# GNN kernel on one core: propagation and last layer on edge rows, sums per tile of 128 sorted edges by one-hot products, third residual step in the last propagation round, output scattered

## The chip, the cores and the metric

One Trainium2 chip, one of its NeuronCores. The metric is the device time of one execution in microseconds, median of several runs; the kernel before takes 13,499.98 us (three runs, 13,473.8 to 13,504.35). Engines: TensorE (PE), VectorE (DVE), ScalarE (ACT), GpSimd (POOL), and SyncE (SP), which here only issues transfers. Indirect DMAs, which gather or scatter 128 rows by 128 indices held in SBUF, are issued by POOL.

## The reference

50,000 nodes with 96 features, 50,000 edges sorted by destination `dst`; all in f32. Four residual layers, each on `h = relu(layernorm(x))`:

```python
x = x + L0(h)   # attention over edges: segment_sum(V[src]*score, dst) / segment_sum(score, dst)
x = x + L1(h)   # gated message network, segment_sum by dst, update network, layernorm
x = x + L2(h)   # 16 rounds of propagation, no weights:
#   deg = segment_sum(1, dst) + 1 ; norm = rsqrt(deg)[src] * rsqrt(deg)[dst], self loops included
#   g = h ; 16 times: g = 0.9 * segment_sum(norm * g[src], dst) + 0.1 * h
x = x + L3(h)   # deg3 = segment_sum(w, dst) + 1 ; dinv = rsqrt(deg3)
#   y = h @ W ; out = dinv * (segment_sum(w * (dinv*y)[src], dst) + dinv*y) + b
```

The sums by `dst` are what the change is about. About 31,600 nodes have at least one incoming edge; the others get nothing but their self loop.

## The kernel before

Rows of nodes and of edges are laid out alike: 128 partitions with 392 consecutive rows each (`P`, `CH`), so a partition holds a stretch of the sorted edges. Work goes in `NB` = 49 batches of `J` = 8 columns; one indirect DMA moves one column, that is 128 rows of 96 values, so a pass over all edges (or nodes) is 392 of them. `skewed()` writes each engine's program as ticks: in tick t a stage with lag L handles batch t - L, the stages in the order given; four batches are in flight. Between stages of the program stands a `Block`, at whose ends all engines meet.

Sums along a partition (`scan_step`, lines 344 to 359): for each of the eight columns VectorE runs two `scalar_tensor_tensor`, a running sum `S` that restarts where `dst` changes, and a sum `F` over the edges whose `dst` is that of the partition's first edge. `F` is needed where a segment crosses partitions: after the last batch a product with the matrix `B` adds up what the partitions before contribute, and 128 extra rows (`AUX`) hold it. A node finds its sum by a pointer (`ptr_i`, for layer 2 `yptr_i`), which is another gather.

The stages, with the lines that matter:

- Preparation (from 380): masks, counts and weights per edge, the slots of each segment; while layer 0's node products run, 392 scatters write `info_t` (556).
- Layer 0 and layer 1: edge stages with `scan_step`, node stages that gather the sums (`n_ag`). Layer 1's node stage (1060 to 1226) stores `x2` and the scaled `h` as the start of the propagation, in both `y_t` tables.
- First propagation step (1229 to 1345): per batch 8 gathers of neighbours' values `r_g` and 8 of the edge's own start `r_c`, scan, four VectorE instructions of 128x768; the start term goes to `c_t`, the values stay in SBUF (`H`) and go to `y_t`. An edge row holds the value of its destination node, so a round needs no read-back by nodes: row e of `y_t` is what the sum of the edges up to e gives, and only the last edge of a segment has the full one. `yptr_e` points every edge to it.
- Fifteen rounds (1347 to 1477): POOL gathers, VectorE scans, TensorE adds `H`, `c_t` and the sums in PSUM through the identity (1415, 1416, 1421), ScalarE scales by `k_e` into `H` (1443), SP stores to the other `y_t` (1381). A round begins when all rows of the last are stored (`after(pool, s_st, 16 * NB * r)`).
- Layer 3 preparation (p6, from 1480): gathers of the final values by node `n_y`, `x3 = x2 + root * y`, layernorm, product with `W`, times `dinv` into `z_t`.
- Layer 3 sums (p7): gathers `e_g` of `z_t` by `src`, times weight, scan, into `agg3_t`.
- Output (p8): gathers `n_ag` of the sums by node, plus `z`, times `dinv`, plus `x3` and `b`, stored to `out`.

What orders the rounds on the side of the gathers is this helper, and nothing else is on POOL's queue:

```python
def gathers(table, to, h, done):
    G.sem_inc(s_turn_p)
    for j in range(J):
        G.indirect_dma_start(out=to(j), out_offset=None, in_=table,
                             in_offset=bass.IndirectOffsetOnAxis(ap=idx_s[:, h, j:j + 1], axis=0)
                             ).then_inc(done, 16)
```

## Time and profile before

| | |
|---|---|
| median of the runs | 13,499.98 us |
| span of the profiled execution | 13,552.9 us |
| POOL busy | 9,980.6 us (74%) |
| VectorE busy | 6,176.6 us (46%) |
| TensorE busy, matmul | 6,161.5 us (45%) |
| ScalarE busy | 3,099.7 us (23%) |
| DMA engines, mean | 115 GB/s |

The page gives each engine's busy time and, in 40 slices, how it is spread. The groups of instructions name a line, an engine and an operation with count, busy time, mean length of one, and the idle time just before them with what ended it; "issue" means that nothing in the profile was waited for. The timeline gives single instructions with their start and length in us.

### The profile page before, as it was taken

How to read it: one execution, taken by the hardware profiler on the slowest of the kernel's cores; microseconds unless marked ns; L12 is line 12 of the kernel's file. 1: busy time of each engine (PE TensorE's matmuls, PEld its weight loads, DVE VectorE, ACT ScalarE, POOL GpSimd, SP SyncE). 2: the span in 40 equal slices, each digit the busy share in tenths (PEclk: the TensorE clock that was granted, in tenths of full speed). 3: DMA queues.
4: the chain of work that ended last, by engine and by line, in shares of the span. 5: the costliest groups of instructions: out<-in, count | busy, mean ns of one | idle time of the engine just before them, and what ended most of it. 6: DMA issues, size and time to landing. Idle time of an engine off the chain costs nothing. (4 is left out here: it accounts for less than half of the span.)

```text
span 13552.9 us, 124135 instructions
## 1 busy us (share of the span) xinstructions
PE 6161.5 (45%) x16702; PEld 3564.8 (26%) x16702; DVE 6176.6 (46%) x21955; ACT 3099.7 (23%) x11470; POOL 9980.6 (74%) x10210
## 2 busy tenths in 40 slices
PE   6422105873002555555555555555555555544000
PEld 4322103542001322223323332323322322233000
DVE  4344455596343444444444444444444444444533
ACT  5300133394000222222222222222222222233000
POOL 7677777676777777777777777777777777777777
PEclk8655557886555777777777777777777777755555
DMA  5433353374223333333333333333333333344245
GB/s 150 120 99 100 109 145 97 92 216 142 76 75 89 117 112 112 118 112 112 116 112 112 118 112 112 116 112 112 117 112 112 116 113 112 116 132 129 73 116 140
DMA packets 855833, 1558.86 MB, mean 115 GB/s; under 512 B 321698, under 2 KB 378674, under 8 KB 855666
## 3 DMA queue, kind: packets, MB, share of 16 engines
q1 hardware_dynamic: 523217, 1053.28, 22.9%
q0 software_dynamic: 332448, 504.04, 16.3%
q14 instruction: 148, 1.20, 0.0%
q8 instruction: 20, 0.33, 0.0%
HBM read 954.90 MB, written 602.08 MB: 115 GB/s over the span
## 5 line engine op out<-in xcount | busy, mean ns | idle before, releaser
L340 POOL DMA_INDIRECT r_g<-y_t,idx_s x6272 | 6051.0, 965 | 2128.7 <-issue 2115.0
L349 DVE SCALAR_TENSOR_TENSOR r_S<-r_S,scan_s,r_g 128x96 f32<-128x96 f32 x6272 | 2020.3, 322 | 4670.1 <-DMA r_g<-y_t,idx_s 3968.8
L1421 PE MATMUL r_pu<-r_S,ident 128*128 128x384 f32 x2940 | 1883.7, 787 | 3127.9 <-DVE F L351 3127.9
L1443 ACT ACTIVATE H<-r_pu,k_e 128x96 f32 (+1 forms) x5880 | 1443.3, 356 | 6059.3 <-PE r_pu L1421 6059.3
L351 DVE SCALAR_TENSOR_TENSOR F<-r_g,scan_s,F 128x96 f32<-128x96 f32 x6272 | 1967.6, 314 | 0.0
L1421 PEld LDWEIGHTS r_pu<-r_S,ident 128*128 128x128 f32 x2940 | 737.9, 276 | 3947.0 <-DVE F L351 3583.5
L1415 PE MATMUL r_pu<-H,ident 128*128 (+1 forms) x2940 | 1633.0, 646 | 101.5 <-DMA r_c<-c_t 101.5
L340 POOL DMA_INDIRECT n_ag<-agg_t,idx_s x1176 | 1227.2, 1044 | 395.8 <-issue 368.4
L1416 PE MATMUL r_pu<-r_c,ident 128*128 128x384 f32 x2940 | 1441.4, 578 | 0.0
L1415 PEld LDWEIGHTS r_pu<-H,ident 128*128 128x128 f32 x2940 | 824.4, 281 | 816.9 <-issue 683.4
L1416 PEld LDWEIGHTS r_pu<-r_c,ident 128*128 128x128 f32 x2940 | 712.4, 242 | 599.2 <-issue 383.0
L340 POOL DMA_INDIRECT e_g<-z_t,idx_s x392 | 397.2, 1013 | 148.5 <-issue 120.8
L340 POOL DMA_INDIRECT n_y<-y_t,idx_s x392 | 403.0, 1028 | 135.4 <-issue 118.0
L751 PE MATMUL e_eo<-w_e,e_eaT 97*128 97x96 f32 x784 | 182.7, 428 | 676.3 <-ACT e_eaT L772 676.3
L1297 PE MATMUL r_pc<-r_S,B 128*128 128x96 f32 x2 | 0.7, 475 | 1059.9 <-DVE H L1342 1059.9
L556 POOL DMA_INDIRECT info_t<-seg_s,idx_s x392 | 382.1, 975 | 120.2 <-issue 119.2
L1289 POOL DMA_INDIRECT r_c<-y_t,r_dst_s x392 | 378.0, 964 | 119.5 <-issue 119.5
L340 POOL DMA_INDIRECT e_kv<-kv_t,idx_s x392 | 377.9, 964 | 119.4 <-issue 119.4
L340 POOL DMA_INDIRECT e_x<-rec_t,idx_s x392 | 375.4, 958 | 119.4 <-issue 117.0
L731 POOL DMA_INDIRECT e_q<-q_t,dst_s x392 | 371.2, 947 | 119.5 <-issue 114.3
L349 DVE SCALAR_TENSOR_TENSOR e_S<-e_S,scan_s,e_g 128x96 f32<-128x96 f32 (+1 forms) x1176 | 380.3, 323 | 58.0 <-DVE e_g L800 9.4
L351 DVE SCALAR_TENSOR_TENSOR F<-e_g,scan_s,F 128x96 f32<-128x96 f32 (+1 forms) x1176 | 375.6, 319 | 0.0
(233 smaller groups left out, 7251.4 us busy)
## 6 DMA issues: line engine op xcount, KB each, us to landing
y_t<-H SPq DMA_DIRECT2D x784, 384.0 KB, 2.4
r_c<-c_t SPq DMA_DIRECT2D x735, 384.0 KB
r_g<-y_t,idx_s POOLq DMA_INDIRECT x6272
n_x<-x_t SPq DMA_DIRECT2D x147, 384.0 KB, 4.5
kv_t<-n_kvq SPq DMA_DIRECT2D x49, 768.0 KB, 3.7
agg_t<-e_S SPq DMA_DIRECT2D x98, 384.0 KB, 2.6
x_t<-n_x SPq DMA_DIRECT2D x98, 384.0 KB, 2.4
y_t<-n_y SPq DMA_DIRECT2D x98, 384.0 KB
```

The source lines that it names most:

```text
L340: G.indirect_dma_start(out=to(j), out_offset=None, in_=table, in_offset=bass.IndirectOffsetOnAxis(ap=idx_s[:, h, j:j + 1], axis=0)).then_i ...
L349: own.add(V.scalar_tensor_tensor(out=S[:, h % slots, j, 0:w], in0=before, scalar=scan_s[:, h, j, 0:1], in1=g[:, j, 0:w], op0=ALU.mult, op1 ...
L351: last = V.scalar_tensor_tensor(out=F[:, 0:w], in0=g[:, j, 0:w], scalar=scan_s[:, h, j, 1:2], in1=F[:, 0:w], op0=ALU.mult, op1=ALU.add)
L556: G.indirect_dma_start(out=info_t, out_offset=bass.IndirectOffsetOnAxis(ap=idx_s[:, h, j:j + 1], axis=0), in_=seg_s[:, h, j, :], in_offset ...
L731: G.indirect_dma_start(out=gq[:, h, j, :], out_offset=None, in_=q_t, in_offset=bass.IndirectOffsetOnAxis(ap=dst_s[:, h, j:j + 1], axis=0)) ...
L751: last = T.matmul(eo[g][:, j, :], eaT[:, h, g, j * P:(j + 1) * P], w_e[:], start=True, stop=True)
L1289: G.indirect_dma_start(out=cs[:, h, j, :], out_offset=None, in_=y_t[0][0:ROWS, :], in_offset=bass.IndirectOffsetOnAxis(ap=dst_s[:, h, j:j ...
L1297: T.matmul(pc[:], B[:], S[:, 0, J - 1, :], start=True, stop=True).then_inc(s_cr, 1)
L1415: T.matmul(pu[h % 2][g][:], ident[:], cols(H, b)[:, c, :], start=True, stop=False)
L1416: T.matmul(pu[h % 2][g][:], ident[:], cs[:, h % 2, c, :], start=False, stop=False)
L1421: last = T.matmul(pu[h % 2][g][:], ident[:], S[:, h % 2, 4 * g:4 * g + 4, :], start=False, stop=True)
L1443: last = A.activation(v[:, j, :], pu[h % 2][j // 4][:, j % 4, :], ACT.Copy, scale=k[:, j:j + 1])
```

## The change

The edge side of layers 2 and 3 is laid out anew: a tile is 128 consecutive edges across the partitions, 392 tiles in 49 batches of eight. For each edge its segment's first edge within the tile is known (`start_e`). The sum of a segment is then a product of the tile's rows with a one-hot matrix built by comparing a ramp with `start_e`; every edge's column picks the row of its segment's representative. A segment that continues from the tile before is carried by a second product with a matrix that is zero but for column 0 (`pass_e`), whose moving operand is the finished sum of the tile before; both add up in one of four PSUM banks and ScalarE copies the result to SBUF, where the next carried product reads it. The scan, `F`, `B`, the extra rows and the values kept in SBUF are gone in these stages.

- A new block before everything loads `dst`, `src` and weights by tiles, works out starts, passes, representatives and output rows, and turns them so that an edge is a partition. After layer 1 a small block turns the pointers (`row_e`).
- The starts `y`, the residual `x2` and four factors of a node lie in one row `yx_t` of 196 values, stored by layer 1's node stage.
- The tables `y_t` and `z_t` hold nodes in their first half and edge rows in the second; each edge knows the row of its source.
- The first step gathers `y` by source and `yx` by destination (8 and 8 per batch). In the same stage layer 3's preparation runs over all nodes as if they had no incoming edge, and writes their output to `out`.
- Fifteen rounds follow, fourteen of them as above. The last, the fifteenth after the first step, also does the third residual step and layer 3's preparation on edge rows.
- Layer 3's sums and output are one stage: gather, weigh, product, finish, and 392 scatters of output rows; rows that are not representatives carry an index out of bounds and are dropped.

The stages p6, p7 and p8 of before are gone. The diff, cut to its core:

```diff
-        def pointers(own, ptr, no, start, t, to, base):
+        with ExitStack() as pt:
+            ...
+                    load_tiles(sp, di, dst, N, s_in)
+                    load_tiles(sp, ni, dst[1:N], N - 1, s_in)
+                    load_tiles(sp, si, src, N, s_in)
+                    load_tiles(sp, wt, edge_weight, N, s_in)
+                    ...
+                    for k, a in enumerate((sf, wt, df, dg, st, cc, rp)):
+                        ...
+                        for c in range(4):
+                            last = T.transpose(tb[k][:, c * P:(c + 1) * P], a[:, c, :], ident[:])
+                        last.then_inc(s_tb, 1)
...
+        def onehot(b, to):
+            return V.tensor_tensor(to, iota_f[:].unsqueeze(1).to_broadcast([P, J, P]),
+                                   cols(start_e, b).unsqueeze(2).to_broadcast([P, J, P]), ALU.is_equal)
+
+        def segments(pe, turn, first, h, E, C, g, S, bank, s_ev, s_po):
+            def own_tile(j):
+                after(pe, s_ev, J * turn + j - TB + 1)
+                alone = first and j == 0
+                ins = T.matmul(bank[j % TB][:], E[:, h % 2, j, :], g[:, j, 0:D], start=True, stop=alone)
+                ...
+            def carried(j):
+                ...
+                after(pe, s_ev, J * turn + j)
+                before = S[:, (h - 1) % 2, J - 1, :] if j == 0 else S[:, h % 2, j - 1, :]
+                T.matmul(bank[j % TB][:], C[:, h % 2, j, :], before, start=False, stop=True).then_inc(s_po, 1)
+            own_tile(0)
+            for j in range(1, J):
+                own_tile(j)
+                carried(j - 1)
+            carried(J - 1)
+
+        def evacuate(act, turn, h, S, bank, s_po, s_ev):
+            for j in range(J):
+                after(act, s_po, J * turn + j + 1)
+                A.copy(S[:, h % 2, j, :], bank[j % TB][:]).then_inc(s_ev, 1)
...
 first step, VectorE
+                    skewed(dve, (0, marks), (2, scale), (1, begin), (1, value), (1, add), (4, finish))
...
 rounds, SyncE
+                            after(sp, s_b, r * NB + b - 3)
+                            sp.sem_inc(s_turn_s)
+                            sp.dma_start(yo[:, h], rows_of(y_t[odd], ROWS, b)).then_inc(s_ld[h], 16)
+                            sp.dma_start(cs[:, h], rows_of(c_t, 0, b)).then_inc(s_ld[h], 16)
 rounds, GpSimd
-                        after(pool, s_st, 16 * NB * r)
-                        after(pool, s_zo, 16 * r)
-                        pool.sem_inc(s_turn_p)
+                        for h in range(K):
+                            after(pool, s_st[h], 16 * OF[h] * r)
+                            pool.sem_inc(s_turn_p)
+                        def step(b, n, h):
+                            after(pool, s_ix, r * NB + b + 1)
+                            after(pool, s_po, J * (r * NB + b - 3))
+                            gathers(y_t[odd], lambda j: g_[:, h, j, :], h, s_g[h])
 rounds, VectorE
-                            scan_step(dve, own, h, D, g_[:, h % GB], S, 2, s_ss, r * NB + b + 1)
+                    def marks(r):
+                        def run(b, n, h):
+                            after(dve, s_po, J * (r * NB + b - 1))
+                            onehot(b, E[:, h % 2]).then_inc(s_e, 1)
+                            V.tensor_copy(C[:, h % 2, :, 0], cols(pass_e, b)).then_inc(s_cc, 1)
+                    def begin(r):
+                            dve.wait_ge(s_ld[h], 32 * (r * OF[h] + n + 1))
+                            V.tensor_tensor(bt[:, h % 2], yo[:, h], cs[:, h], ALU.add).then_inc(s_b, 1)
+                    def value(r):
+                            ...
+                            after(dve, s_ev, J * (r * NB + b + 1))
+                            after(dve, s_b, r * NB + b + 1)
+                            own.do(V.tensor_tensor(ys[:, h], S[:, h % 2], bt[:, h % 2], ALU.add))
+                            V.tensor_tensor(ys[:, h], ys[:, h], wide(kc_e, b, 0), ALU.mult).then_inc(s_y, 1)
+                    def one(r, odd):
+                        skewed(dve, (0, marks(r)), (1, begin(r)), (1, value(r)))
 last round
+                        skewed(act, (-2, slots(LAST)), (1, sums(LAST)), (3, norm), (4, turned),
+                               (2, lambda b, n, h: ln_root(act, b, mv[:, h], rn[:, h], s_mv, s_sd)))
+                        skewed(pe, (1, sums(LAST)), (5, product), (4, turn))
+                        skewed(dve, (0, marks(LAST)), (1, begin(LAST)), (1, value(LAST)), (3, scale), (5, weigh), (2, add))
...
 layer 3 sums and output
+                            G.indirect_dma_start(
+                                out=out, out_offset=bass.IndirectOffsetOnAxis(ap=dst_s[:, h, j:j + 1], axis=0),
+                                in_=ot[:, h, j, :], in_offset=None, bounds_check=bound, oob_is_err=False
+                            ).then_inc(s_d[h], 16)
+                    skewed(pool, (0, step), (2, scatter))
+                    skewed(dve, (0, marks), (1, weigh), (1, finish))
```

## Rows read from the trace of the kernel before

**Rows 1.** The page, busy us by engine, and the granted clock in tenths.

```profile
PE 6161.5 (45%) x16702; PEld 3564.8 (26%) x16702; DVE 6176.6 (46%) x21955; ACT 3099.7 (23%) x11470; POOL 9980.6 (74%) x10210
PEclk8655557886555777777777777777777777755555
```

**Rows 2.** Tile `info_t`, POOL's scatters: ns min/median/max, first and last start in us.

```profile
L556 POOL DMA_INDIRECT info_t<-seg_s,idx_s x392: 972/974/1307, 31.9 to 532.3; - x196
```

**Rows 3.** Tiles `r_g` (propagation) and `e_g` (layer 3), the same columns.

```profile
L340 POOL DMA_INDIRECT r_g<-y_t,idx_s x6272: 941/947/1732, 3234.6 to 11910.6; - x196
...
L340 POOL DMA_INDIRECT e_g<-z_t,idx_s x392: 942/947/1731, 12474.0 to 12994.7; - x196
```

**Rows 4.** Timeline (start us, us, engine, line): first round's first gather, and its end.

```profile
4270.12 0.95 POOL L340 DMA_INDIRECT r_g<-y_t,idx_s  x1 [12.13 <-ACT scan_s L1437]
...
4763.80 0.95 POOL L340 DMA_INDIRECT r_g<-y_t,idx_s  x1 [0.31 <-issue]
...
4766.40 0.32 DVE L349 SCALAR_TENSOR_TENSOR r_S<-r_S,scan_s,r_g 128x96 f32<-128x96 f32 x1 [5.50 <-DMA r_g<-y_t,idx_s]
...
4775.18 0.35 SPq L1381 DMA_DIRECT2D y_t<-H  x1
...
4778.77 0.95 POOL L340 DMA_INDIRECT r_g<-y_t,idx_s  x1 [14.03 <-issue]
```

**Rows 5.** POOL's groups (busy us, mean ns, idle): a round, then p6, p7, p8.

```profile
L340 POOL DMA_INDIRECT r_g<-y_t,idx_s x392 | 376.1, 959 | 133.2 <-issue 133.2
...
L340 POOL DMA_INDIRECT n_y<-y_t,idx_s x392 | 403.0, 1028 | 135.4 <-issue 118.0 <-ACT idx_s L1557 17.4
...
L340 POOL DMA_INDIRECT e_g<-z_t,idx_s x392 | 397.2, 1013 | 148.5 <-issue 120.8 <-ACT scan_s L1631 27.8
...
L340 POOL DMA_INDIRECT n_ag<-agg_t,idx_s x389 | 405.2, 1042 | 125.8 <-issue 121.8 <-ACT idx_s L335 4.0
```

**Rows 6.** Timeline in p6 and p8, VectorE and POOL.

```profile
12004.18 0.96 DVE L1533 TENSOR_TENSOR n_x<-n_x,n_y 128x768 f32<-128x768 f32 x1
12004.40 1.55 POOL L340 DMA_INDIRECT n_y<-y_t,idx_s  x1 [0.30 <-issue]
...
13099.14 0.95 DVE L1709 TENSOR_TENSOR n_x<-n_x,r_all 128x768 f32<-128x768 f32 x1
13099.48 1.43 POOL L340 DMA_INDIRECT n_ag<-agg_t,idx_s  x1 [0.30 <-issue]
```

**Rows 7.** Busy us by engine, PEclk, DMA share, GB/s: a round; layer 1's nodes.

```profile
4786.00:5296.00 510.00, 293.23 (x590) 151.51 (x590) 217.67 (x788) 105.92 (x490) 376.12 (x393) 0.79 0.38 114
2770.00:2880.00 110.00, 86.73 (x418) 56.11 (x419) 102.90 (x469) 104.84 (x236) 84.69 (x84) 0.89 0.76 221
```

**Rows 8.** Timeline of TensorE: sixteen halves in a row; a lone product and its reader.

```profile
12001.23 3.72 PE L1586 MATMUL n_po<-w,n_hT 96*128 96x96 f32 x16 [5.52 <-ACT n_hT L1567]
...
13002.83 0.74 PE L1624 MATMUL e_pc<-e_S,B 128*128 128x96 f32 x2 [535.07 <-DVE F L351]
13003.71 0.25 DVE L1652 TENSOR_TENSOR Z<-F,e_pc 128x96 f32<-128x96 f32 x1 [0.94 <-PE e_pc L1624]
```

**Rows 9.** Groups of ScalarE that read PSUM: 96, 288 and 512 columns.

```profile
L1443 ACT ACTIVATE H<-r_pu,k_e 128x96 f32 x4320 | 1060.4, 356 | 4301.4 <-PE r_pu L1421 4301.4
...
L600 ACT COPY n_kvq<-n_ob 128x288 f32<-128x288 f32 x196 | 72.2, 392 | 90.9 <-PE n_ob L628 90.9
...
L1006 ACT COPY e_xT<-e_tp 128x512 f32<-128x512 f32 x98 | 52.9, 588 | 12.9 <-PE e_tp L962 11.3 <-issue 1.5
```

**Rows 10.** VectorE: a group of 128x768, and eight statistics in the timeline.

```profile
L1529 DVE TENSOR_TENSOR n_y<-n_y,root 128x768 f32<-128x768 f32 x49 | 47.4, 967 | 235.9 <-DMA n_y<-y_t,idx_s 235.9
...
12005.17 1.38 DVE L306 BATCH_NORM_STATS2 n_st<-n_x 128x6 f32<-128x96 f32 x8
12006.69 0.64 DVE L311 BATCH_NORM_AGGREGATE n_mv<-n_st 128x2 f32<-128x6 f32 x8
```

More of the change, by code:

```diff
@@ L1621, in _, with sums, run @@
+                    one.eng = pool
+                    rounds(one, lambda: one(LAST, 0))
                 @block.tensor
                 def _(pe):
-                    pe.wait_ge(s_s[0], PAIRS + 1)
-                    T.matmul(pc[:], B[:], S[:, 0, J - 1, :], start=True, stop=True).then_inc(s_cr, 1)
+                    def sums(r):
+                        def run(b, n, h):
+                            turn = r * NB + b
+                            after(pe, s_e, turn + 1)
+                            after(pe, s_cc, turn + 1)
+                            s_g.wait(pe, h, 16 * J * (r * OF[h] + n + 1))
+                            segments(pe, turn, isinstance(b, int) and b == 0, h, E, C, g_[:, h], S, pr, s_ev, s_po)
+                        return run
@@ L1626, in _, with slots, run @@
+                    one.eng = pe
+                    rounds(one, last)
                 @block.scalar
                 def _(act):
-                    def step(n, h):
-                        act.wait_ge(s_s[h], n)
-                        gather_slots(act, n, h, src_i, s_ix, s_g, 16 * J)
-                        A.copy(scan_s[:, h], cols(scan, 2 * n + h)).then_inc(s_ix[h], 1)
-                    batches(act, step)
+                    def slots(r):
+                        def run(b, n, h):
+                            s_g.wait(act, h, 16 * J * (r * OF[h] + n))
+                            A.copy(idx_s[:, h, :], cols(row_e, b)).then_inc(s_ix, 1)
+                        return run
@@ new lines, in _, with sums @@
+                    skewed(pool, (0, step), (2, scatter))
+                    for h in range(K):
+                        s_d.wait(pool, h, 16 * J * OF[h])
+                @block.tensor
+                def _(pe):
+                    def sums(b, n, h):
+                        after(pe, s_e, b + 1)
+                        after(pe, s_cc, b + 1)
+                        after(pe, s_w, b + 1)
+                        segments(pe, b, isinstance(b, int) and b == 0, h, E, C, g_[:, h], S, pr, s_ev, s_po)
+                    skewed(pe, (1, sums))
@@ new lines, in finish @@
+                    def finish(b, n, h):
+                        s_d.wait(dve, h, 16 * J * n)
+                        after(dve, s_ev, J * (b + 1))
+                        dve.wait_ge(s_ld[h], 32 * (n + 1))
+                        own.step(b)
+                        own.do(V.tensor_tensor(ot[:, h], S[:, h % 2], zo[:, h], ALU.add))
+                        own.do(V.tensor_tensor(ot[:, h], ot[:, h], wide(kc_e, b, 3), ALU.mult))
+                        own.end()
+                        V.tensor_tensor(ot[:, h], ot[:, h], x3[:, h], ALU.add).then_inc(s_o, 1)
```

945 lines of the change are left out of this document (533 added, 412 removed).

## Prediction

> **What bounds the kernel now.** I read the page's busy shares first, then the instructions of each engine in order of time, then the groups by tile. POOL is busy 74% of the span, no other engine half [rows 1], and what POOL does is issue indirect DMAs. One gather takes 0.947 us in the median [rows 3], and the gather after it starts 0.30 us later with "issue" as the only reason: inside a stretch the starts lie 1.25 us apart. 392 tiles of 128 rows make a pass of 490 us. Before, there are 26 such passes (10,193 instructions): slots of segments, two for layer 0, its read-back, one for layer 1, its read-back, two for the first propagation step, fifteen steps, and one each for layer 3's preparation, sums and output. Everything else lies beside them, except at the end of a step: from the last gather's start to the next step's first are 14.97 us [rows 4], in which gather, scan, product, ScalarE and store run one after another. A step is (11910.6 - 4763.8) / 14 = 510.5 us [rows 3, 4].
>
> The second thing to see is that the gathers are not always 0.947 us long. Their mean is 0.959 in the propagation, but 1.028, 1.013 and 1.042 in the last three stages [rows 5], and single ones take 1.4 to 1.7 us. Set beside VectorE's instructions these have one cause. At 12004.40 a gather starts while a tensor_tensor with both inputs in SBUF has run since 12004.18 and ends at 12005.14; the gather takes 1.55 us, 0.60 more than normal. At 13099.48 one starts inside a tensor_tensor that ends at 13100.09; it takes 1.43, 0.48 more [rows 6]. Both fit: delay = end of the VectorE instruction - start of the gather - 0.14. The propagation has 16 scan instructions a batch that also read two SBUF operands, but each lasts 0.32 us, which leaves almost nothing to wait for: 0.01 us per gather.
>
> The Trainium skill says this in "SBUF — State Buffer", section "Who interferes with whom": a VectorE instruction with two SBUF inputs and a GpSimd instruction that reads SBUF exclude each other, and the later one waits for the whole of the first. The two pairs agree with it (0.60 and 0.48 us). By this rule the change below pays on POOL; if it did not hold, the sum would be that of the first rival.
>
> **The change, part by part.** My sum stands against the profiled execution's own 13552.9 us; the median is 0.4% lower, and I scale by that at the end.
>
> Number of passes: layer 3's read-back of x and its read-back of sums go, a scatter of the output comes: 25 instead of 26. The gather of starts (784-byte rows now, for 384) stays one pass; I give it the same 0.947 us.
>
> *Preparation.* A new block loads the edges once more in tiles, scans, turns seven arrays and stores one. The same kind of work before the first scatter takes 31.9 us now [rows 2], of which the new block repeats most; some 9 us of vector work and an iota fall away; after layer 1 comes a block of store, load, turn (two DMA landings and a block change, about 14). Layer 1's node stage stores 784-byte rows and has one ScalarE copy more per batch; there ScalarE is busy 104.8 of 110 us [rows 7], so I charge 5. Together +40 (15 to 80).
>
> *The tile sums.* The scan on VectorE goes. Each tile is now a product with a one-hot matrix, plus a second product that carries the last row of the tile before, and a ScalarE copy of the result; the carried product waits for that copy. That is one chain through all 392 tiles of a step. At the lower clock (1.2 GHz) one lone 128x96 f32 product takes 0.74 us, and its consumer starts 0.88 us after it began; in a stream sixteen halves take 3.72, so 0.465 a product [rows 8]. A ScalarE copy from PSUM takes 0.392 at 288 columns and 0.588 at 512, which gives 0.23 at 96; the scaled form takes 0.356 [rows 9]. One link is 0.83 + 0.23 + 0.05 = 1.11 us (1.2 with the longer copy), and the own product of a later tile fits into the copy. A batch is 8 x 1.11 + 0.6 = 9.5 us. At 2.4 GHz it is shorter; the granted clock was 0.79 with TensorE busy 293 of 510 us [rows 7]. So the chain is just under POOL's 10.0 us per batch and I let POOL cover it; where POOL is slower than that the cover grows. By "TensorE: Matmul & The Clock Gate" of the Trainium skill (section "LDWEIGHTS") 128 columns would load in 107 ns; no half product here comes at less than 0.23 us at this clock, and the row is used.
>
> *VectorE beside it.* Per batch VectorE now runs the one-hot (1024 wide, about 1.25 us by 0.967 for 768 [rows 10]), a small copy, the sum of starts, and two instructions on the values: 4.1 us of tensor_tensor with both inputs in SBUF. They stand back to back: the two on values wait for the end of the chain, then comes the mark of the batch after next and the next sum of starts, none of which waits. With gathers 1.25 us apart: one that starts in the first 0.8 us waits 0.4 on average for the end of the first instruction, the next starts at 2.1 inside the one-hot and waits 1.0, the third falls behind the end: 1.4. From the other phases it is 0.5 to 1.0. The mean over the phases is 1.1 us. What rows show: 0.54 a batch for one such instruction (8 x (1.013 - 0.945)), 0.66 for two, 0.78 for four [rows 5]. I take 1.06 in place of 0.11 now: +0.95 per batch; bounds +0.4 and +1.65 (best and worst phase).
>
> *End of a step.* POOL waits on four semaphores for the stores of the step. To the landing 2.6 us [rows 4], chain 9.3, two vector instructions 2.0, then 3.6 from store to gather as now: 17.6 for 14.97, +2.6. Queued behind that wait are only the next step's gathers, and all engines wait for these.
>
> *Fourteen steps:* 14 x (49 x 0.95 + 2.6) = +690 (+275 to +1,200).
>
> *First step.* 784 gathers x 1.25 = 980, plus 8.0 us of such vector work per batch, at 0.28 us of delay per us 2.2, x 49 = 108, plus an end of 37 (chain, norm, products, output of the last batches). Before: 3234.6 to 4270.1 = 1035.5 [rows 3, 4]. +90 (30 to 150). The dense work of the nodes is hidden under two gathers per row.
>
> *Last step with layer 3's preparation.* Here the cover is gone. ScalarE does eight copies, norm, turned copies and the root in order, and the root waits for statistics that VectorE reaches only after values 2.0, scale 0.4, weights (which wait for the products, to 4.3), residual 2.0, statistics 1.4 and 0.64 [rows 10]: 7.6 to 8.4 us after the last copy. Only then go the next eight copies: 6.3 to 8 + 7.6 to 8.4 = 15.3 us per batch, x 49 = 750, + 27 = 777. Before: from the fifteenth step's start (11910.6 - 493.7 = 11417) to layer 3's first gather at 12474.0 [rows 3] = 1057. -280 (-480 if POOL sets it, -190). SP's loads of x and stores of x and z, moved here, stand behind the store of y and are not late.
>
> *Layer 3's sums and output.* 392 gathers at 1.25 and 392 scatters at 0.974 + 0.30 [rows 2] = 992, 5.1 us of such vector work per batch gives 1.3 x 49 = 64, ends 25: 1081. Before 13552.9 - 12474.0 = 1079 [rows 3]. 0 (-60 to +60).
>
> DMA: one load of 384 KB more per batch of a step, from a busy share of 0.38 [rows 7] to about 0.5; hidden.
>
> Sum: +40 + 90 + 690 - 280 + 0 = +540: 14,093, scaled by 13,500 / 13,553: **14,040 us**. Its own range, by the bounds of the vector delay, is 13,620 to 14,560.
>
> **Rivals.** *The gathers are not held up more than now* (phases fall well, or the one-hot's repeated operand does not count). For it: the scan instructions hold the same operands and cost 0.1 us a batch; a gather that starts with a vector instruction is not delayed. Against it: 4.1 us without a gap hold three starts. Then 40 - 20 - 35 - 290 - 65 = -370: 13,130. This is the side on which the change is faster: one pass less and one merged. It decides at a net delay of about 0.16 us a batch, where the sum is nought.
>
> *The chain bounds.* If a link takes 1.45 us instead of 1.11 (weights not loaded ahead after the wait, both products in one queue), a batch is 12.2 us, 1.15 over the delayed POOL's 11.05, x 686 = +790: 14,830. For it: two f32 products and two copies' waits in strict order; it decides from a link of 1.31. Against: the lone product's 0.74.
>
> *The change does not do what it says* (a stage left serial by a wait I took for free, such as both one-hot buffers held by the tile count): it would show as a batch above 12 us too and has the second rival's price.
>
> **How the numbers follow.** Forecast 0.68; no added delay 0.18; chain or a serial wait 0.14. The range 13,200 to 14,600 takes in most of the near side of the first rival and the forecast's bounds; outside stay half of the first rival and most of the second. A measurement of this kernel tells about 0.2% from no change. Faster 0.20 (first rival and the lowest phases), within 0.2% 0.03, slower 0.77.
>
> **What would show it.** Right: gathers of the steps with a mean near 1.07 to 1.1 us and single ones of 1.5 to 1.9 that end with a tensor_tensor; a step of 550 to 570 us; POOL never waiting inside a step; batches of 14 to 17 us in the last one. Wrong: a mean of 0.96 with steps near 510 (first rival), or POOL waiting for tile sums and starts of chains 11 us and more apart (second). The preparation is wrong if the first scatter starts outside 45 to 80 us.

## The result, and the profile after

The changed kernel takes 14,071.75 us (14,064.23 to 14,086.94), the kernel before beside it 13,502.17: a ratio of 1.0427, 95% interval 1.0414 to 1.0440. It is 4.3% slower. 14,040 was forecast.

The page of the changed kernel, the lines that answer to [rows 1]; its span is 14,069.3 us:

```profile
PE 9222.9 (66%) x35678; PEld 7687.3 (55%) x35678; DVE 5843.8 (42%) x13580; ACT 3392.5 (24%) x12008; POOL 10275.9 (73%) x9818
...
PEclk7655558885555555555555555555555555555555
```

POOL has 392 instructions fewer and is busy 295 us longer. TensorE has risen from 45% to 66%, and yet its clock stays at the lower level through the fourteen middle rounds (mean granted clock 0.50 of 2.4 GHz), where it was granted 0.78 before.

Where the steps begin: tiles `info_t`, `r_g`, `e_g` (as [rows 2, 3]), then the first gathers of the first, the second and the last round.

```profile
L660 POOL DMA_INDIRECT info_t<-seg_s,idx_s x392: 971/972/1306, 56.0 to 555.6; - x196
...
L348 POOL DMA_INDIRECT r_g<-y_t,idx_s x6272: 938/944/1977, 3258.5 to 12941.1; - x196
...
L348 POOL DMA_INDIRECT e_g<-z_t,idx_s x392: 939/947/1819, 13018.7 to 14027.8; - x196
```

```profile
4404.95 0.94 POOL L348 DMA_INDIRECT r_g<-y_t,idx_s  x1 [43.90 <-ACT idx_s L1741]
...
4971.70 0.94 POOL L348 DMA_INDIRECT r_g<-y_t,idx_s  x1 [18.38 <-issue]
...
12206.49 0.94 POOL L348 DMA_INDIRECT r_g<-y_t,idx_s  x1 [17.84 <-issue]
```

From these and from [rows 3, 4] the account by stages, in us:

| stage | before | after | difference | forecast |
|---|---|---|---|---|
| up to the first `r_g` | 3,234.6 | 3,258.5 | +24 | +40 |
| first step | 1,035.5 | 1,146.5 | +111 | +90 |
| fourteen steps | 7,146 | 7,801.5 | +656 | +690 |
| last step (with layer 3's preparation) | 1,058 | 812.2 | -246 | -280 |
| layer 3, sums and output | 1,079 | 1,050.6 | -28 | 0 |
| sum | | | +517 | +540 |

A round is 557.3 us in the mean of fourteen (510.4 before). POOL's groups over the whole run (line, engine, tiles, count, busy us, mean ns, idle before):

```profile
L348 POOL DMA_INDIRECT r_g<-y_t,idx_s x6272 | 6684.7, 1066 | 2491.7 <-issue 2108.3 <-ACT idx_s L1741 163.8 <-PE r_pr L1390 141.2
...
L348 POOL DMA_INDIRECT e_g<-z_t,idx_s x392 | 413.8, 1056 | 195.8 <-issue 118.8 <-ACT idx_s L1900 76.7 <-PE e_pr L1390 0.3
L1879 POOL DMA_INDIRECT out<-e_o,e_out_s x392 | 389.2, 993 | 119.4 <-issue 119.4
```

The median gather is 0.944 us as before, the mean 1.066: few gathers carry all the delay. One batch in the middle of a round shows which (timeline: start, length, engine, line; in brackets the idle time before):

```profile
6001.35 0.24 ACT L1400 COPY r_S<-r_pr 128x96 f32<-128x96 f32 x1 [0.83 <-PE r_pr L1390]
...
6001.62 0.96 DVE L1798 TENSOR_TENSOR r_y<-r_S,r_b 128x768 f32<-128x768 f32 x1 [7.28 <-ACT r_S L1400]
6002.01 1.39 POOL L348 DMA_INDIRECT r_g<-y_t,idx_s  x1 [0.30 <-issue]
6002.71 0.96 DVE L1800 TENSOR_TENSOR r_y<-r_y,kc_e 128x768 f32<-128x768 f32 x1
...
6003.49 1.16 PE L1381 MATMUL r_pr<-r_g,r_E 128*128 128x96 f32 x4 [2.17 <-DMA r_g<-y_t,idx_s]
6003.59 1.22 DVE L1368 TENSOR_TENSOR r_E<-iota_f,start_e 128x1024 f32<-128x1024 f32 x1
6003.71 1.92 POOL L348 DMA_INDIRECT r_g<-y_t,idx_s  x1 [0.30 <-issue]
```

The last copy of a batch (6001.35) releases the values. The gather of 6002.01 lies inside the first of them (end 6002.58) and takes 1.39; that of 6003.71 lies inside the one-hot (end 6004.81) and takes 1.92. By the forecast's formula they should be delayed by 0.43 and 0.96; they are by 0.45 and 0.98. The others have 0.94. Not every batch is like this one: of the 686 batches of the fourteen rounds 282 have two held gathers, 390 have one and 14 none. TensorE, for its part, stood idle 2.17 us waiting for gathers: the chain is not what sets the batch here.

The formula can be put to all 5,488 gathers of these rounds. 940 start at least 0.05 us after the start of a wide tensor_tensor and more than 0.2 us before its end; each of them is delayed by what the formula gives, 0.007 to 0.031 us more. 123 start within 0.05 us of the instruction's start, and of these only 6 are held. The 4,363 that start inside no tensor_tensor take 0.962 us at most. The one-hot makes up 409 of the 692 us of delay.

### The profile page after: what moved, and what is told of

It is laid out like the page before. It is cut to its first block and busy times, and to the rows that moved or that the text cites. A ratio compares the mean times of both kernels' runs of the same rounds, so it can differ in the third digit from the quotient of the medians.

```text
span 14069.3 us, 157719 instructions
## 1 busy us (share of the span) xinstructions
PE 9222.9 (66%) x35678; PEld 7687.3 (55%) x35678; DVE 5843.8 (42%) x13580; ACT 3392.5 (24%) x12008; POOL 10275.9 (73%) x9818
## 5 line engine op out<-in xcount | busy, mean ns | idle before, releaser
L348 POOL DMA_INDIRECT r_g<-y_t,idx_s x6272 | 6684.7, 1066 | 2491.7 <-issue 2108.3
L1390 PE MATMUL r_pr<-r_S,r_C 128*128 128x96 f32 x12512 | 4541.4, 466 | 824.5 <-ACT r_S L1400 794.7
L1381 PE MATMUL r_pr<-r_g,r_E 128*128 128x96 f32 x12544 | 3856.4, 424 | 1629.7 <-DMA r_g<-y_t,idx_s 1629.7
L1381 PEld LDWEIGHTS r_pr<-r_g,r_E 128*128 128x128 f32 x12544 | 3288.1, 329 | 1794.1 <-issue 1781.9
L1390 PEld LDWEIGHTS r_pr<-r_S,r_C 128*128 128x128 f32 x12512 | 3155.7, 313 | 1689.1 <-ACT r_S L1400 1011.8
L1400 ACT COPY r_S<-r_pr 128x96 f32<-128x96 f32 x6272 | 1493.2, 238 | 6938.7 <-PE r_pr L1390 6672.8
L1798 DVE TENSOR_TENSOR r_y<-r_S,r_b 128x768 f32<-128x768 f32 x735 | 708.3, 964 | 5153.1 <-ACT r_S L1400 5153.1
L1368 DVE TENSOR_TENSOR r_E<-iota_f,start_e 128x1024 f32<-128x1024 f32 x784 | 954.1, 1217 | 0.2 <-issue 0.2
L1800 DVE TENSOR_TENSOR r_y<-r_y,kc_e 128x768 f32<-128x768 f32 x735 | 706.9, 962 | 90.7 <-DVE r_y L1798 26.0
L1786 DVE TENSOR_TENSOR r_b<-r_yo,r_c 128x768 f32<-128x768 f32 x735 | 705.5, 960 | 73.8 <-DMA r_c<-c_t 73.8
```

Of the source, the lines that this page charges most:

```text
L348: G.indirect_dma_start(out=to(j), out_offset=None, in_=table, in_offset=bass.IndirectOffsetOnAxis(ap=idx_s[:, h, j:j + 1], axis=0)).then_i ...
L1368: return V.tensor_tensor(to, iota_f[:].unsqueeze(1).to_broadcast([P, J, P]), cols(start_e, b).unsqueeze(2).to_broadcast([P, J, P]), ALU.is ...
L1381: ins = T.matmul(bank[j % TB][:], E[:, h % 2, j, :], g[:, j, 0:D], start=True, stop=alone)
L1390: T.matmul(bank[j % TB][:], C[:, h % 2, j, :], before, start=False, stop=True).then_inc(s_po, 1)
L1400: A.copy(S[:, h % 2, j, :], bank[j % TB][:]).then_inc(s_ev, 1)
L1786: V.tensor_tensor(bt[:, h % 2], yo[:, h], cs[:, h], ALU.add).then_inc(s_b, 1)
```

## The experiments

Times by batch are differences between the starts of each batch's first gather over the fourteen rounds; their median was 10.10 us before and 10.80 after (means 10.12 and 11.00). The hold of a batch is what its eight gathers take over 0.944 us each, added up.

**Does one such instruction cost this, without the rest of the change?** Into the rounds of the kernel before, after the last scan of each batch:

```diff
+                            V.tensor_tensor(extra[:], ident[:, 0:D].unsqueeze(1).to_broadcast([P, J, D]),
+                                            cols(k_e, b).unsqueeze(2).to_broadcast([P, J, D]), ALU.is_equal)
```

> The kernel before with one more VectorE instruction per batch of a round, after the last scan: a tensor_tensor of 128x768 with both inputs in SBUF, into a tile that nobody reads. Theory (a gather that starts inside such an instruction waits for its end less 0.14 us): the last scan follows a gather's start by 3.25 us (4763.80 to 4767.05), so the added instruction of 0.967 us lies 0.75 to 1.72 us after a start on a grid of 1.25 us; one gather a batch is held 1.72 - 1.25 - 0.14 = 0.33 us; 735 batches give +240 us, 13,740 (0.0 to 0.83 a batch by the phase, so 13,500 to 14,110). Single gathers of 1.3 to 1.8 us in the rounds, one a batch. Rival (gathers are not held up, VectorE is off the path): 13,500.

Measured: 13,833.57 us against 13,456.83, ratio 1.0278 (1.0261 to 1.0295). 377 us over 735 batches are 0.51 a batch: the kind was right and the rival (no effect) falls. The phase was not. The 3.25 us in the expectation reach only to the batch's first scans; its last one ends at 4771.03, 7.2 us after that gather's start. In this run a gather starts 0.15 to 0.25 us after the added instruction in 467 of the 686 batches of fourteen rounds, and is held by 0.6 to 0.7 us and not 0.33. The same place with one input instead:

```diff
+                            V.tensor_scalar(extra[:], ident[:, 0:D].unsqueeze(1).to_broadcast([P, J, D]), 1.0, None,
+                                            ALU.is_equal)
```

> The same place and the same 768 columns, but a tensor_scalar with one input in SBUF and a constant. Theory (only two SBUF inputs hold a gather): 13,500 within 30 us, gathers of the rounds at a mean of 0.96 as before. Rival (any VectorE instruction beside a gather holds it for its length): it lasts about 0.6 us, so 0 to 0.45 a batch and 13,500 to 13,830, with gathers of over 1.2 us once a batch.

Measured: 13,555.28 us, ratio 1.0072 (1.0055 to 1.0089), 98 us more. The theory falls: it is not free. The time lies low in the rival's range (0 to 330 us more), but gathers of over 1.2 us come in 70 of 686 batches and not in each. The timeline shows the same rule at work on a shorter instruction:

```profile
6199.88 0.56 DVE L1464 TENSOR_SCALAR r_extra<-ident 128x768 f32<-128x768 f32 x1
...
6200.15 1.10 POOL L340 DMA_INDIRECT r_g<-y_t,idx_s  x1 [0.30 <-issue]
```

End less start less 0.14 is 0.15; the gather takes 0.16 more than 0.94. Over the rounds 669 gathers start inside the added instruction and are held by 0.135 us in the mean, where the formula gives 0.125. So two inputs are not the condition; here a wide instruction with one input holds a gather too. The Trainium skill allows for it in "SBUF — State Buffer", section "Who interferes with whom": `tensor_scalar` can run in a mode that takes both port pairs, and then it excludes GpSimd as well. 0.56 us for 768 columns, where two inputs take 0.96, fits such a mode; no run here shows the mode itself.

**The one-hot without two inputs**, in the changed kernel:

```diff
-            return V.tensor_tensor(to, iota_f[:].unsqueeze(1).to_broadcast([P, J, P]),
-                                   cols(start_e, b).unsqueeze(2).to_broadcast([P, J, P]), ALU.is_equal)
+            for j in range(J):
+                last = V.tensor_scalar(to[:, j, :], iota_f[:], cols(start_e, b)[:, j:j + 1], None, ALU.is_equal)
+            return last
```

> The changed kernel with the one-hot matrix built by eight tensor_scalar of 128x128 (ramp compared with one value per partition: one SBUF input) in place of one tensor_tensor of 128x1024, in all three stages. Nothing else. Theory (two-input hold): the gather of 1.92 us in each batch, which starts inside the one-hot, falls to 0.94 to 1.4; per batch 0.5 to 1.0 us less, rounds of 557 become 510 to 535, in all 14,072 - 14 x 22..47 and some 30 to 60 from the two other stages: 13,350 to 13,750, likeliest 13,600. Rival (the chain of carried products sets the batch, gathers only look long): 14,050 to 14,100. Rival (any VectorE instruction holds a gather): the eight take longer in sum (1.7 us for 1.22), so 14,072 or more.

Measured: 13,546.55 us, ratio to the kernel before 1.0067 (1.0050 to 1.0084): 525 us below the changed kernel (by each one's own runs of before, (1.0427 - 1.0067) x 13,480 = 485 us). The batch is 10.35 us (mean 10.37), a round 526.5, the first step 1,093. This lies inside the expected range, and it is the decisive run. Chain, products, clock (0.50 granted in the rounds) and transfers are untouched, VectorE works longer, and five sixths of the loss are gone. The mean hold of a batch falls by 0.63 us, from 1.01 to 0.38, and the mean batch by the same 0.63. The chain did not set the batch.

```profile
6200.02 1.65 DVE L1369 TENSOR_SCALAR r_E<-iota_f,start_e 128x128 f32<-128x128 f32 x8
...
6200.13 0.98 POOL L348 DMA_INDIRECT r_g<-y_t,idx_s  x1 [0.30 <-issue]
...
6201.42 1.06 POOL L348 DMA_INDIRECT r_g<-y_t,idx_s  x1 [0.31 <-issue]
```

The gather of 6200.13 starts inside a string of eight that runs until 6201.67 and is delayed by 0.04 us: between short one-input pieces it gets through. So do the others: 1,154 gathers of the fourteen rounds start inside such strings, and they are held by 0.05 us in the mean and 0.13 at most. Do short two-input pieces let it through as well?

**All four wide instructions of the rounds in eight pieces**, each with two inputs as before, for instance:

```diff
-                            V.tensor_tensor(bt[:, h % 2], yo[:, h], cs[:, h], ALU.add).then_inc(s_b, 1)
+                            for j in range(J):
+                                last = V.tensor_tensor(bt[:, h % 2, j, :], yo[:, h, j, :], cs[:, h, j, :], ALU.add)
+                            last.then_inc(s_b, 1)
```

> The changed kernel with the four wide VectorE instructions of the rounds (one-hot, start sum, value sum, value product) each cut into eight of 128x128 or 128x96, all still with two SBUF inputs. VectorE's busy time per batch about doubles (4.1 to some 8 us). Theory (a held gather waits for the end of the one instruction it meets, not for the sum): the longest piece is 0.3 us, a hold at most 0.16, so gathers at a mean of 0.96 to 1.0, rounds at 515 to 530, in all 13,450 to 13,700. Rival (what counts is the share of time in which VectorE reads two operands): gathers at 1.15 or more and 14,150 or more. Rival (chain bounds): 14,072 plus up to 14 x 4 for the longer vector part at the end of a round.

Measured: 14,289.55 us, ratio 1.0616 (1.0598 to 1.0633). My theory falls in this point: a round is 570.0, the gathers have a mean of 1.094, and the time is in the range of the first rival (14,150 or more), though its mean of 1.15 for the gathers is not reached.

```profile
6206.68 1.44 DVE L1804 TENSOR_TENSOR r_y<-r_S,r_b 128x96 f32<-128x96 f32 x8 [5.36 <-ACT r_S L1400]
...
6207.44 0.99 POOL L348 DMA_INDIRECT r_g<-y_t,idx_s  x1 [0.30 <-issue]
...
6209.51 1.70 DVE L1780 TENSOR_TENSOR r_E<-iota_f,start_e 128x128 f32<-128x128 f32 x8
...
6210.03 2.00 POOL L348 DMA_INDIRECT r_g<-y_t,idx_s  x1 [0.30 <-issue]
```

The second gather waited 1.06 us, to 0.12 before the end of the whole string (6211.21), not of the piece that it met. But the first one starts inside a string of the same kind and is held by 0.05 us only, so a string does not simply act as one instruction. Of the gathers that start in one of the first six pieces of the two strings on values (1,003 in fourteen rounds), none is held by more than 0.12 us. Of the 590 that start inside the string of the one-hot 280 wait to its end and 297 are held by less than 0.1. And 153 of the 196 that start in the last two pieces of the value product wait until the one-hot behind it has ended. Together a batch is held by 1.25 us, 0.24 more than by the four wide instructions, and the mean batch is 0.24 longer. When a string lets a gather in is left open. The scan instructions of the kernel before are nearly as short and each pair waits for the one before; they hold a gather by 0.1 us at most.

**Experiments on a chip with pauses.** Some kernels ran on a chip where the kernel before took 15,997 us, 19% more than elsewhere, and where the traces of the others show pauses, up to 30 us on VectorE, in engines that had nothing to wait for. Their times are not comparable with the rest. One is the changed kernel without the carried products in the fourteen rounds, so that sums over two tiles are wrong:

> The changed kernel without the carried products in the fourteen rounds: every tile's sum is its own product alone, so that segments over two tiles get a wrong sum; all waits, copies and VectorE instructions stay. There is then no chain between tiles. Theory (POOL with its held gathers sets the batch, the chain of 8.6 us fits beside it): inside a round nothing changes but the phase in which VectorE meets gathers (plus or minus 0.3 us a batch); at the end of each round the last eight tiles come out 3 to 5 us sooner: 14,072 - 14 x 4 = 14,015 (13,800 to 14,220 with the phases). Rival (the chain sets the batch): the batch falls to 10.0 us, 14,072 - 14 x 49 x 1.0 = 13,390.

Measured 15,849.83 against 15,997.0, ratio 0.9913 (0.9897 to 0.9930), with batches from 10.0 to 14.7 us (tenth and ninetieth hundredth): nothing follows for the chain. The longer link is told below from another chip (here 17,191.87, ratio 1.0741). Two more changed the orders of the last round, the second together with the one-hot by scalars. Beside the edit shown, VectorE makes the scale ahead of the values:

```diff
-                        skewed(act, (-2, slots(LAST)), (1, sums(LAST)), (3, norm), (4, turned),
-                               (2, lambda b, n, h: ln_root(act, b, mv[:, h], rn[:, h], s_mv, s_sd)))
+                        skewed(act, (-2, slots(LAST)), (3, lambda b, n, h: ln_root(act, b, mv[:, h], rn[:, h], s_mv, s_sd)),
+                               (1, sums(LAST)), (3, norm), (4, turned))
```

> The changed kernel with two orders changed in the last round alone: ScalarE takes the root of the batch before last ahead of the eight copies instead of after everything, and VectorE makes the scale from it ahead of the values. The serial loop (eight copies 7.5, values 2.0, weights 1.3, residual, statistics, root: 15.85 us a batch) is cut; what is left in one engine is ScalarE: root 0.3, copies 7.7, norm 3.0, turned copies 1.1 = 12.2 us. Theory: the last step 812 becomes 49 x 12.4 + 30 = 640, in all 14,072 - 170 = 13,900 (13,850 to 13,960). Rival (the last step is bound by TensorE or by the loads of x): 14,072. Rival (POOL): 11.0 a batch, 13,830.

> The changed kernel with both: the one-hot by scalars (13,547 alone, 525 less) and the orders of the last round. If the two causes are separate stages of the time they add up: 14,072 - 525 - 170 + 0..20 = 13,380 (13,320 to 13,430), which is below the kernel before (13,457 in the last call). If the gain in the last round was already taken by the first edit (its POOL time was not on the path there, so it should not be): 13,547.

Measured 16,350.16 (ratio 1.0211) and 17,639.89 (ratio 1.1037). These times say nothing, but the trace of the first shows a mistake in the edit: the batch of the last round is 15.8 us in the median, after the change it was 16.0.

```profile
15063.06 0.64 DVE L319 BATCH_NORM_AGGREGATE l_mv<-l_st 128x2 f32<-128x6 f32 x8 [0.15 <-DVE l_st L314]
...
15063.74 0.30 ACT L324 ACTIVATE l_rn<-l_mv,eps 128x8 f32<-128x8 f32 x1 [2.57 <-DVE l_mv L319]
15063.94 0.22 ACT L1400 COPY r_S<-r_pr 128x96 f32<-128x96 f32 x1
```

The root, now ahead of the copies, waits for statistics that are made at the end of the tick before, and the copies wait behind it. The loop is the same one, entered at another point.

**The loop cut.** With the one-hot by scalars, the root goes directly behind the copies, the turns ahead of the products, the scale ahead of the values:

```diff
+                        skewed(act, (-2, slots(LAST)), (1, sums(LAST)),
+                               (3, lambda b, n, h: ln_root(act, b, mv[:, h], rn[:, h], s_mv, s_sd)),
+                               (3, norm), (4, turned))
...
+                        skewed(pe, (1, sums(LAST)), (4, turn), (5, product))
...
+                        skewed(dve, (0, marks(LAST)), (1, begin(LAST)), (3, scale), (1, value(LAST)), (2, add), (5, weigh))
```

> The one-hot by scalars, and other orders in the last round: on ScalarE the root of the batch before last directly behind the eight copies (the root ahead of the copies had left the loop closed: it waited for statistics made at the end of the tick before), on TensorE the turns ahead of the products, on VectorE the scale ahead of the values and the weights last. Theory (the last step's 15.9 us a batch is a serial loop through four engines): what is left is TensorE at its lower clock, chain 8.6 + turns 1.7 + products 3.6 = 13.9 us; the step falls from 815 to 49 x 14.1 + 30 = 720, in all 0.7% below the one-hot by scalars alone, which was 1.0067 of the kernel before: ratio 1.000 (0.996 to 1.004), 13,455 where the kernel before takes 13,457. Rival (DMA or POOL sets the last step): 1.0067.

Measured: 13,377.66 us, ratio 0.9941 (0.9924 to 0.9957). This version beats the changed kernel by 694 us (655 by each one's own runs of before) and the kernel before by 0.6%. The last step is 634.6 us instead of 814.9, more than expected. The batches there are of two kinds, 13.8 us and 10.8 to 12.5. In windows of the last round (length; busy us of PE, PEld, DVE, ACT, POOL; granted clock; DMA share; GB/s):

```profile
11830.00:11880.00 50.00, 48.69 (x204) 44.44 (x204) 36.55 (x117) 22.75 (x75) 35.56 (x34) 0.50 0.57 186
11880.00:11930.00 50.00, 48.06 (x215) 43.30 (x215) 39.29 (x138) 21.82 (x73) 30.72 (x29) 0.57 0.50 161
11930.00:11980.00 50.00, 41.45 (x252) 36.45 (x251) 46.23 (x152) 28.13 (x93) 37.02 (x36) 0.84 0.65 216
```

At the lower clock TensorE is busy 48.7 of 50 us and sets 13.8 us a batch, the 13.9 of the expectation. Then the clock rises, a link goes from 1.07 to 0.79 us, and VectorE is the busiest, 46 of 50. Over this last round the mean granted clock was 0.68.

**Values tile by tile.** In addition, in the first step and the rounds:

```diff
+            for j in range(J):
+                after(dve, s_ev, J * turn + j + 1)
+                V.scalar_tensor_tensor(out=ys[:, h, j, :], in0=S[:, h % 2, j, :], scalar=cols(kc_e, b)[:, j, 0:1],
+                                       in1=bt[:, h % 2, j, :], op0=ALU.mult, op1=ALU.add).then_inc(s_y, 1)
```

> As the run above, and the values made tile by tile beside the chain: in the first step and the rounds eight scalar_tensor_tensor of 128x96 (tile sum times factor, plus start), each waiting only for its own tile's copy, in place of two instructions of 128x768 after the last copy; the start sum has its own value weighed by eight tensor_scalar and then one addition, so per batch of a round two of four wide two-input instructions are left as one. Theory: 1.07 us apart, pieces of 0.3 us hold a gather at most 0.16 us; the batch falls from 10.37 to 10.1 us, the end of a round by 1.6 us: 14 x (49 x 0.25 + 1.6) = 190, 30 in the first step: 220 less than the run above, ratio 0.984 to the kernel before (0.978 to 0.992). Rival (eight short two-input pieces hold as much as one wide one, as eight pieces without gaps did): no gain or up to 1% more than the run above.

Measured: 13,394.67 us, ratio 0.9955 (0.9939 to 0.9972); not told apart from the run above, against an expected ratio of 0.984. By stages: first step 1,061.5 (1,094.6), rounds 525.8 (527.4), last step 695.4 (634.6). At the end of a round it gains 1.3 of the 1.6 us. Within a round it gains nothing: the hold of a batch is 0.40 us in both runs. The scalar_tensor_tensor pieces add almost nothing to it (14 us in all), but the one wide instruction left, the start's sum, now stands where gathers meet it: 625 start inside it where 188 did, and it makes up 0.31 of the 0.40. In the last round TensorE is busy nearly all the time at the lower clock:

```profile
11940.00:11990.00 50.00, 49.02 (x202) 44.49 (x201) 44.37 (x183) 21.08 (x70) 30.18 (x30) 0.50 0.54 176
```

Its batches there are 13.8 us, as at the lower clock in the run above; the mean granted clock of the round was 0.55.

> The two last kernels put together: values tile by tile in the first step and the fourteen rounds, wide values and the other orders in the last round. By the stages' own times: 13,378 with the first step at 1,062 instead of 1,095 and the rounds at 525.8 instead of 527.4: 13,378 - 33 - 22 = 13,323, ratio 0.990 (0.987 to 0.993). If the last round depends on how the values are made before it, or VectorE is late there with one wide instruction more behind the chain, 0.994 to 0.996.

Measured: 13,386.41 us, ratio 0.9929 (0.9913 to 0.9946), again not told apart. The last step is 692.6 although its values are wide again, so it was not the values that cost the 61 us. Its batches are mostly 13.8 us: the mean granted clock of this round was 0.56, for 0.68 where the step took 634.6. Why the clock rose in the one and not in the others is open.

**A longer link in the chain.** The changed kernel with one more copy per link:

```diff
+                    A.copy(via[:, j % 2, :], bank[j % TB][:]).then_inc(s_via, 1)
+                    act.wait_ge(s_via, J * turn + j + 1)
+                    A.copy(S[:, h % 2, j, :], via[:, j % 2, :]).then_inc(s_ev, 1)
```

> The changed kernel with one more copy in every link of the chain, in the fifteen rounds: ScalarE copies a tile's sum to a small tile, waits for that, and copies it on. The link becomes 1.07 + 0.24 + about 0.1 = 1.4 us, above the 1.31 from which the chain was said to decide, a batch 8 x 1.4 + 0.6 = 11.8 us against 11.0 now. Theory: POOL now waits in each batch for tile sums, fourteen rounds of 557 become 49 x 11.8 + 19.5 + 2.7 - 11 = 590, the last step grows by 49 x 8 x 0.34 = 133: 14,072 + 14 x 33 + 133 = 14,670 (14,450 to 14,850). If POOL's delays were added to the chain rather than hidden beside it, the whole 49 x 8 x 0.34 x 15 = 2,000 would come: 16,070. If the link had slack beside TensorE's own products: 14,072 to 14,200.

> The changed kernel with one more copy in every link of the chain in the fifteen rounds, once more, because all kernels of that call, the one before too, stood still at times. Theory (POOL with its held gathers and the chain run beside each other, the longer one counts; the chain decides from a link of 1.31 us): link 1.07 + 0.35 = 1.42, batch 8 x 1.42 + 0.6 = 12.0 against 11.04 now, fourteen rounds 14 x (46 x 0.95 + 3) = 655 more, the last step 49 x 2.8 = 137 more: 14,072 + 790 = 14,860, ratio to the kernel before 1.101 (1.09 to 1.11). Rival (delays add up): 16,070, ratio 1.19. Rival (slack in the link): 1.043.

Measured, on an undisturbed chip: 14,323.36 us, ratio 1.0621 (1.0603 to 1.0638).

```profile
7009.50 0.24 ACT L1401 COPY r_via<-r_pr 128x96 f32<-128x96 f32 x1 [0.83 <-PE r_pr L1390]
7009.77 0.27 ACT L1403 COPY r_S<-r_via 128x96 f32<-128x96 f32 x1
...
7010.10 0.74 PE L1390 MATMUL r_pr<-r_S,r_C 128*128 128x96 f32 x2 [0.20 <-ACT r_S L1403]
...
7010.87 0.24 ACT L1401 COPY r_via<-r_pr 128x96 f32<-128x96 f32 x1 [0.83 <-PE r_pr L1390]
```

The link is 1.37 us (7009.50 to 7010.87), and the mean batch 11.15. The expected 12.0 came from a link of 1.42 and a pause of 0.6 between two batches of the chain. There is no such pause: the chain's shortest batches take 10.99 us, 8 x 1.37.

That is just under the 11.00 that a batch took with the short link, so the chain would decide only from a link of about 1.37 (an estimate, 11.00 / 8), and here it does not clearly decide yet. In 671 of 672 batches POOL waited nowhere for more than 0.1 us beyond its usual 0.30, and the 0.15 us by which the batch is longer are hold: 1.155 for 1.01. The instructions that hold the gathers are released by the chain, so a later chain moves them; that this is why the hold grew is only argued. A round is 9.8 us longer, 7 of them by the hold and 2.7 at its end, 137 in all. The last step, where nothing covers the link, grows by 111. Neither full addition (ratio 1.19) nor the expected 1.101 came, but a little over the 1.043 of a link with slack. Where the chain begins to decide was not reached.

## Why the prediction was right

**What bounds.** POOL's issue of indirect DMAs, lengthened by VectorE's instructions: a_two_inputs and c_onehot_scalars show it from both sides, one adds it to the kernel before, the other takes the largest piece out of the changed one. All runs on undisturbed chips agree (means over the fourteen rounds, us):

| run | hold of a batch | batch | difference |
|---|---|---|---|
| before | 0.13 | 10.12 | 9.99 |
| b_one_input | 0.20 | 10.20 | 9.99 |
| c_onehot_scalars | 0.38 | 10.37 | 9.99 |
| j_orders, k_tiles | 0.40 | 10.39 | 9.99 |
| l_best | 0.41 | 10.40 | 9.99 |
| a_two_inputs | 0.60 | 10.59 | 9.99 |
| after | 1.01 | 11.00 | 9.99 |
| long_link_again | 1.155 | 11.15 | 9.99 |
| d_pieces | 1.25 | 11.24 | 9.99 |

In all ten kernels a batch inside a round is 9.99 us, eight gathers at their undisturbed 1.25 us, plus what these are held. The granted clock was 0.76 to 0.78 in the rounds of the kernel before and its two variants and 0.50 in the others; it makes no difference here.

**Fourteen steps, +690 forecast, +656 measured.** The hold was put at 1.06 us a batch for 0.11 before; it is 1.01 for 0.13. The 1.1 that the forecast calls the mean over the phases does not follow from the values beside it (1.4, and 0.5 to 1.0), but it is right: its formula, worked over all phases of four instructions of these lengths, gives 1.17 (an estimate). The steady batch has one held gather more often than two, so the phases are not spread evenly, and that the mean came out so near is in part luck. The mean batch rose by 0.88: 0.88 x 48 x 14 = 591 us, and 13 for the gathers of each round's last batch. The end of a step was 17.6 in the forecast for 14.97. The row of 14.97 lies below the mean: from a step's last gather to the next one's first it is 15.7 us before and 19.4 after, 52 in fourteen steps where 36 were forecast. Together these are 656. The bounds of this term are slightly off too: 14 x (49 x 0.4 + 2.6) is 311 and not 275, and with 1.65 it is 1,168 and not 1,200.

One end of a round:

```profile
4952.37 0.95 POOL L348 DMA_INDIRECT r_g<-y_t,idx_s  x1 [0.30 <-issue]
...
4956.43 1.14 PE L1381 MATMUL r_pr<-r_g,r_E 128*128 128x96 f32 x4 [3.71 <-DMA r_g<-y_t,idx_s]
...
4965.58 0.24 ACT L1400 COPY r_S<-r_pr 128x96 f32<-128x96 f32 x1 [0.83 <-PE r_pr L1390]
4965.91 0.96 DVE L1798 TENSOR_TENSOR r_y<-r_S,r_b 128x768 f32<-128x768 f32 x1 [10.01 <-ACT r_S L1400]
...
4971.70 0.94 POOL L348 DMA_INDIRECT r_g<-y_t,idx_s  x1 [18.38 <-issue]
```

Chain (4956.43 to 4965.82, 9.4 for 9.3) and values (2.0) are as worked out, store to gather 3.8 for 3.6; but the last gather lands 4.06 us after its start, for 2.6 taken from [rows 4] (in the mean of fourteen 3.7 for 2.45). The queues are fuller by one load a batch (DMA share 0.46 for 0.38 in the rounds), which I had called hidden. It is hidden inside the step; that it is what delays the last landing is only argued.

**The link.** 1.11 us forecast; 1.07 measured (0.83 from product to copy, 0.24 the copy, the next product in the same moment). The lone product's row [rows 8] gave it. The lower clock, on which it depended, held through the fourteen rounds. The 0.6 between two batches is not there (10.99 = 8 x 1.37 in long_link_again), so the chain alone would have taken 8.6 us and not 9.5.

**First step, +90 for +111.** Its holds come to (1.188 + 1.016 - 2 x 0.947) x 392 = 122 us, for the 108 worked out from 8.0 us of vector work a batch:

```profile
L1480 POOL DMA_INDIRECT r_yx<-yx_t,r_dst_s x392 | 465.8, 1188 | 119.4 <-issue 119.4
L348 POOL DMA_INDIRECT r_g<-y_t,idx_s x392 | 398.2, 1016 | 197.3 <-issue 115.5 <-ACT r_dst_s L1517 78.1 <-PE r_pr L1390 3.7
```

The rest is the end of the step. With the one-hot by scalars the step falls by 53.

**Last step, -280 for -246.** The serial loop is there: copies 7.5, then 8.4 to the next copy, 15.9 a batch for 15.3. j_orders shows that it was the order that made it, and g_root_first that an order can be changed without cutting the loop.

**Preparation and layer 3.** The first scatter starts at 56.0, inside 45 to 80, so +24 there; after layer 1 nothing is lost on balance, where 14 and 5 us were charged. Layer 3 came out 28 us shorter; its gathers and scatters are held 0.11 and 0.02 us each in the mean (1.056 for 0.947, 0.993 for 0.972), 51 of the 64 us that were forecast, and the ends took about 10 us for 25 (392 gathers and 392 scatters without holds are 989 us, not 992).

**The rivals.** "Not held up more than now" is refuted by the holds of all gathers (1.01 for 0.13), "the chain bounds" by c_onehot_scalars. Its price was too high: without the 0.6 a link of 1.45 would give a batch of 11.6 us (an estimate, 8 x 1.45), 0.6 and not 1.15 over POOL's.

**The sum.** By stages the measured changes less the forecast ones are -16, +21, -34, +34 and -28 us. These add up to -23. So the mechanism and the size of each term were right, but that the total came within 0.3% is luck.

## What to carry to other kernels

If GpSimd issues the DMAs that bound a kernel, count every wide VectorE instruction as a possible hold of an issue that starts while it runs, by its end less the issue's start. What worked was form and size together: a comparison with one value per partition (one tensor input, short pieces) in place of a wide one with two gave 525 us; the same work cut into short two-input pieces without gaps made it worse. Moving instructions about can undo such a gain: in k_tiles the one wide instruction left met three times as many gathers.

When a stage loses its cover, follow its engines around one tick: an instruction moved along the same loop changes nothing, one moved behind what it doesn't need cuts it (180 us here, 122 in l_best, where the clock stayed mostly low).

## What the runs showed of the hardware

- An indirect DMA whose issue starts inside a wide `tensor_tensor` with two SBUF inputs waits until 0.13 us before that instruction's end (940 gathers, all within 0.02 us of this); one that starts within 0.05 us of its start is mostly not held (117 of 123).
- A wide `tensor_scalar` with one SBUF input holds it too (0.56 us long, 1.10 for 0.94); a string of 128-column ones with a value per partition holds it by 0.13 us at most (0.98 in the rows shown).
- Two-input `tensor_tensor` pieces without a gap hold some gathers to the end of the string and beyond (2.00 and up to 2.86 us for one gather) and let others in at once (0.99).
- TensorE's clock stayed at 1.2 GHz through 7,800 us in which it was busy 0.77 of the time, and at that level also while it was busy 48.7 of 50 us; in the last round of j_orders the mean granted clock of the next windows rose to 0.57 and 0.84, with busy shares of 0.96 and 0.83. The Trainium skill says in "TensorE: Matmul & The Clock Gate", section "Part 1: The HAM clock gate", that the level follows how busy the array has been; by the busy shares in these rows alone the level can't be told.
